# First attention of a gated cross-attention network on one core: the order of a unit's transposes and its products with V

## The chip, the cores and the metric

The kernel runs on one core of one Trainium2 chip. The time is that of one execution on the device, in microseconds (us). The engines are TensorE (PE in the profile; PEld is its loading of weights), VectorE (DVE), ScalarE (ACT), GpSimd (POOL) and SyncE (SP), which here only starts transfers. All of them run their own streams of instructions and wait for one another on semaphores that the program sets by hand.

## The reference

Four layers are computed one after the other, each added to x; the change touches the first attention only. It has 32 heads over 8 key-value heads, queries of 256 rows and keys of 768 rows, in two batches.

```python
kv = jnp.concatenate([context, latents], axis=1)
q = (latents @ Wq).reshape(bsz, q_len, HEADS, HEAD_DIM).transpose(0, 2, 1, 3)
k = (kv @ Wk).reshape(bsz, kv_len, KV_HEADS, HEAD_DIM).transpose(0, 2, 1, 3)
v = (kv @ Wv).reshape(bsz, kv_len, KV_HEADS, HEAD_DIM).transpose(0, 2, 1, 3)
q = rms_norm(q, q_norm_w)
k = rms_norm(k, k_norm_w)
scores = jnp.einsum('bhgqd,bhkd->bhgqk', qg, k) * scale
probs = jax.nn.softmax(scores.astype(jnp.float32), axis=-1).astype(q.dtype)
out = jnp.einsum('bhgqk,bhkd->bhgqd', probs, v)
...
x = x + jnp.tanh(g_xattn[0]) * _L0_xattn_ref(_layernorm(x, axis=-1), ctx_4096, ...)
```

## The kernel before, in words

Each fp32 product is made of three matmuls (`mm3`, L72 to L74): every operand is kept as a high part (`...H`, written by ACT) and a low part (`...L`, what the high part leaves out, written by DVE).

The first attention makes one turn for each of the 8 key-value heads g. A turn has 8 units u: head u // 2 of the group's four, batch u % 2. What is done for a unit, with the short names that the text uses:

- S(u): scores of unit u, 12 matmuls into the two banks `score0` and `score1`, half a unit (a query tile of 128) in each. DVE takes the maximum of each half (L443), ACT the exponential of each half (L316), into `probs`.
- T(u, j), j = 0, 1, 2: four transposes of `probs` for a third of the keys, into one bank `tbank` (L539). ACT copies the bank into `ptH` (L290; here hi(u, j)); DVE then writes `ptL` from the bank and `ptH` (L430; here lo(u, j)). The bank is free when lo(u, j) has ended.
- V(u, j): six matmuls of that third with V into `obank`.
- Q(h): four transposes of the queries of the next head, into a `tbank`, at the start of even units; `qTH` by ACT, `qTL` by DVE (L432).
- R(h): four transposes of the reciprocals of the row sums of head h, into a `tbank`. ACT copies them to `o_norm` (`factors`), DVE multiplies the head's output by them (`normalise_o`, L456), ACT copies that to `oTH` (`hi_o`, L310), POOL makes `oTL` from it (`o_lo_part`, L205).

PE's order in a unit u of `attend` is Q or R where there is one, S(u + 1), and then T(u, 0) V(u - 1, 0) T(u, 1) V(u - 1, 1) T(u, 2) V(u - 1, 2). ACT's is the copies of Q or R, hi(u, 0), an exponential, hi(u, 1), an exponential, `hi_o` in odd units from 3 on, hi(u, 2). DVE's is shown below. There are two `tbank`s, used in turn through one list `order`, and each set of transposes waits for the low part of the set two before it. There are two `obank`s, one for each second head.

At the end of a turn PE projects the queries of the next turn (`project_q`), with one tile of it ahead of the last unit's V. Its weights are split into high and low parts by POOL, which works in this order in a turn: `o_lo_part` of head 0, split of `wo`, `o_lo_part` of head 1, split of `wq` (for which SP loads the stage once `wo` has been split out of it), split of `wkv`, the rest. After it PE goes through the projections of keys and values, the transposes of K and the output product of the turn.

Of the kernel before, what the change touches and what calls it, by code (L numbers as in the profile page):

```python
# [18 lines left out]
fp32 = mybir.dt.float32  # L19
f32r = mybir.dt.float32r  # L20
bf16 = mybir.dt.bfloat16
ALU = mybir.AluOpType
ACT = mybir.ActivationFunctionType
# [22 lines left out]
def f32(ap):  # L46
    return ap.bitcast(fp32)
# [29 lines left out]
def attn0(nc, S, ctx, A):  # L77
# [23 lines left out]
    vH, vL = sb("vH", [P, NKT, D0], f32r), sb("vL", [P, NKT, D0], f32r)  # L101
    qTH, qTL = sb("qTH", [P, GRP, ROWS], f32r), sb("qTL", [P, GRP, ROWS], f32r)
    kTH, kTL = sb("kTH", [P, NKT * P], f32r), sb("kTL", [P, NKT * P], f32r)
    NP, NPT = 4, 4
    probs_mem = sb("probs", [P, NP * SKV], fp32)
    probs = probs_mem[:].rearrange("p (n k) -> p n k", n=NP)

# [6 lines left out]
    negmax, rsum = sb("negmax", [P, 16], fp32), sb("rsum", [P, 16], fp32)  # L114
    ps = S.psum_in(ctx)
    score = [ps(f"score{i}", [P, 1024], fp32) for i in range(2)]
    tbank = [ps(f"tbank{i}", [P, 512], fp32) for i in range(2)]
    obank = [ps(f"obank{i}", [P, 512], fp32) for i in range(2)]
    pbank = [score[i // 2][:, (i % 2) * 512:(i % 2 + 1) * 512] for i in range(4)]

    U, CH = 2 * GRP, 3
# [2 lines left out]
    for u in range(U):  # L124
        if u % 2 == 0 and u // 2 + 1 < GRP:
            order.append(("q", u // 2 + 1))
        if u % 2 == 1 and u >= 3:
            order.append(("r", (u - 3) // 2))
        order += [("p", CH * u + j) for j in range(CH)]
    order.append(("r", GRP - 1))  # L130
    at = {name: i for i, name in enumerate(order)}
    TC = len(order)
    NS, NKV = 2, NKT // 2
    wq_split, wkv_split, wo_split = S.wq_split, sem("wkv_split"), sem("wo_split")
    pe_q, act_q, pe_kv, act_kv, v_lo = sem("pe_q"), sem("act_q"), sem("pe_kv"), sem("act_kv"), sem("v_lo")
# [3 lines left out]
    Q_NORMED, K_NORMED = RT, [RT + 2 * i + 2 for i in range(3)]  # L139
    pe_t, t_hi, t_lo = sem("pe_t"), sem("t_hi"), sem("t_lo")  # L140
    pe_s, s_max, s_exp, r_inv = sem("pe_s"), sem("s_max"), sem("s_exp"), sem("r_inv")
    pe_pv, o_hi, o_lo = sem("pe_pv"), sem("o_hi"), sem("o_lo")
    pe_wo, x_add = sem("pe_wo"), sem("x_add")
    LAST = KVH - 1

# [6 lines left out]
    with nc.Block() as block:  # L152
# [26 lines left out]
        def _(pool):  # L179
# [7 lines left out]
            def split_wq(g):  # L187
                split(wqH[:], wqL[:], S.wqo_stage[:], S.wq_in, g, wq_split)
# [34 lines left out]
            def turn(g):  # L223

                o_lo_part(g, 0)
                split_wo(g)
                o_lo_part(g, 1)
                pool.wait_ge(pe_q, RT * g + RT)
                split_wq(g + 1)
                pool.wait_ge(pe_kv, NKV * g + NKV)  # L230
                split_wkv(g + 1)
                for h in range(2, GRP):
                    o_lo_part(g, h)
                rsqrt_items(g + 1)

            def last():
# [10 lines left out]
        def _(act):  # L247
# [39 lines left out]
            def hi(g, name, out, scale=1.0):  # L287
                c = at[name]
                act.wait_ge(pe_t, TC * g + c + 1)
                act.activation(out, tbank[c % 2][:], ACT.Copy, scale=scale).then_inc(t_hi, 1)  # L290

            def hi_q(g, h):
                hi(g, ("q", h), qTH[:, h, :], scale=S.wqk[:])
# [12 lines left out]
                hi(g, ("r", h), o_norm[:])  # L306

            def hi_o(g, h):
                act.wait_ge(t_lo, TC * g + at["r", h] + 1)
                act.activation(oTH[:, h, :], o_norm[:], ACT.Copy).then_inc(o_hi, 1)  # L310

            def exp(g, m):
# [6 lines left out]
            def attend(g):  # L319
                exp(g, 0)  # L320
                exp(g, 1)
                for u in range(U):
                    if u % 2 == 0 and u // 2 + 1 < GRP:
                        hi_q(g, u // 2 + 1)
                    if u % 2 == 1 and u >= 3:
                        factors(g, (u - 3) // 2)
                    hi_p(g, CH * u)
                    if u + 1 < U:
                        exp(g, 2 * u + 2)
                    hi_p(g, CH * u + 1)  # L330
                    if u + 1 < U:
                        exp(g, 2 * u + 3)
                    if u % 2 == 1 and u >= 3:
                        hi_o(g, (u - 3) // 2)
                    hi_p(g, CH * u + 2)
# [31 lines left out]
        def _(dve):  # L367
# [58 lines left out]
            def lo(g, name, out, hi, scale=None):  # L426
                c = at[name]
                dve.wait_ge(t_hi, TC * g + c + 1)
                if scale is None:
                    i = dve.tensor_tensor(out, tbank[c % 2][:], f32(hi), ALU.subtract)  # L430
                else:
                    i = dve.scalar_tensor_tensor(out, tbank[c % 2][:], scale, f32(hi), ALU.mult, ALU.subtract)  # L432
                i.then_inc(t_lo, 1)

            def lo_q(g, h):
# [16 lines left out]
            def normalise_o(g, h):  # L452
                c = at["r", h]
                dve.wait_ge(t_hi, TC * g + c + 1)
                dve.wait_ge(pe_pv, 24 * g + 2 * CH * (h + 1))
                dve.tensor_tensor(o_norm[:], obank[h % 2][:], o_norm[:], ALU.mult).then_inc(t_lo, 1)  # L456

            def attend(g):
                for u in range(U):
                    if u + 1 < U:  # L460
                        maximum(g, 2 * u + 2)
                    if u % 2 == 0 and u // 2 + 1 < GRP:
                        lo_q(g, u // 2 + 1)
                    if u % 2 == 1 and u >= 3:
                        normalise_o(g, (u - 3) // 2)
                    if u + 1 < U:
                        maximum(g, 2 * u + 3)
                    for c in range(CH * u, CH * u + CH):
                        lo(g, ("p", c), ptL[:, c % NPT, :], ptH[:, c % NPT, :])
                    if u % 2 == 1:  # L470
                        reciprocals(g, u // 2)

            def add_out(g, t):
                dve.wait_ge(pe_wo, RT * g + t + 1)
                dve.scalar_tensor_tensor(S.X[:, t, :], obank[t % 2][:], S.tanh_g[:, 0:1], S.X[:, t, :],
                                         ALU.mult, ALU.add).then_inc(x_add, 1)

            def turn(g):
# [30 lines left out]
        def _(pe):  # L509
# [23 lines left out]

            def transposes(g, name, ins):
                c = at[name]
                if c >= 2:
                    pe.wait_ge(t_lo, TC * g + c - 1)
                for n, block_in in enumerate(ins):
                    i = pe.transpose(tbank[c % 2][:, n * P:(n + 1) * P], block_in, S.ident[:])  # L539
                i.then_inc(pe_t, 1)  # L540

            def transpose_k(g, i):
# [12 lines left out]
            def scores(g, u):  # L555
                h, b = u // 2, u % 2
                if b == 0 and h:
                    pe.wait_ge(t_lo, TC * g + at["q", h] + 1)
                if h == 0:
                    pe.wait_ge(t_lo, TC * g + at["k", 1 + b] + 1)  # L560
                for m in (2 * u, 2 * u + 1):
                    if u:
                        pe.wait_ge(s_exp, 16 * g + m - 1)
                    q = slice(b * SQ + (m % 2) * P, b * SQ + (m % 2 + 1) * P)
                    for k0, n in ((0, 512), (512, 256)):
                        keys = slice(b * SKV + k0, b * SKV + k0 + n)
                        i = mm3(pe, score[m % 2][:, k0:k0 + n], (qTH[:, h, q], qTL[:, h, q]),
                                (kTH[:, keys], kTL[:, keys]), True, True)
                    i.then_inc(pe_s, 1)
# [7 lines left out]

            def times_v(g, u, j):
                h, b, c = u // 2, u % 2, CH * u + j
                if u % 2 == 0 and j == 0 and h >= 2:  # L580
                    pe.wait_ge(t_lo, TC * g + at["r", h - 2] + 1)
                pe.wait_ge(t_lo, TC * g + at["p", c] + 1)
                for kt in range(2):
                    key = b * KVT + 2 * j + kt
                    part = slice(kt * 256, (kt + 1) * 256)
                    i = mm3(pe, obank[h % 2][:, b * SQ:(b + 1) * SQ], (vH[:, key, :], vL[:, key, :]),
                            (ptH[:, c % NPT, part], ptL[:, c % NPT, part]), j == 0 and kt == 0, j == CH - 1 and kt == 1)
                i.then_inc(pe_pv, 1)

            def attend(g):  # L590

                for u in range(U):
                    if u % 2 == 0 and u // 2 + 1 < GRP:
                        transpose_q(g, u // 2 + 1)
                    if u % 2 == 1 and u >= 3:
                        transpose_factors(g, (u - 3) // 2)
                    if u + 1 < U:
                        scores(g, u + 1)
                    for j in range(CH):
                        transpose_probs(g, u, j)  # L600
                        if u:
                            times_v(g, u - 1, j)

            def finish_units(g):
                for j in range(CH):
                    times_v(g, U - 1, j)
                transpose_factors(g, GRP - 1)

            def output(g, t):
                if t == 0:  # L610
# [3 lines left out]
                    pe.wait_ge(x_add, RT * g + t - 1)  # L614
                rows = slice(t * P, (t + 1) * P)
                for h in range(GRP):
                    i = mm3(pe, obank[t % 2][:], (oTH[:, h, rows], oTL[:, h, rows]),
                            (woH[:, h, :], woL[:, h, :]), h == 0, h == GRP - 1)
                i.then_inc(pe_wo, 1)

# [1015 lines left out]
```

## Time and profile before

| | us |
|---|---|
| median of 3 runs | 1085.82 |
| lowest, highest | 1079.99, 1086.55 |
| the profiled execution's own time | 1088.03 |
| its span in the trace | 1086.2 |
| PE busy | 1005.9 |
| DVE busy | 632.7 |
| ACT busy | 501.4 |
| POOL busy | 359.8 |

The seven turns of the loop repeat every 94 us or so, from about 64 us to 724 us of the span; the eighth stands behind the loop. A row of the timeline gives the start, the duration and, in brackets, how long the engine was idle before it and what released it. The duration of a matmul runs from its start to its modelled end; the next one starts before that, so that the pace is read from the starts. Adjacent instructions on ACT and DVE overlap by about 0.1 us in the same way.

### The profile page before, as it was taken

Reading aid. Unit: us, or ns where it says so; the run is one execution under the profiler, and the core shown is the slowest. Engines: PE = TensorE matmul, PEld = TensorE weight load, DVE = VectorE, ACT = ScalarE, POOL = GpSimd, SP = SyncE. Lnnn points to the kernel's source line nnn. Section 1 sums busy time; section 2 is a strip of 40 time slices with the busy share of each in tenths; the row PEclk is TensorE's granted clock in tenths of the full one; section 3 lists DMA queues with packets and bytes.
Section 4 is the critical chain, followed back from the end, with each engine's and each line's share of the span. In section 5 each row is a group of like instructions: output and inputs, shape, how many; then the busy total and the mean of one; then the engine's idle time right before and its main releaser. Section 6 shows DMA issues by size and latency. Waiting matters only on the chain. (4 is left out here: it accounts for less than half of the span.)

```text
span 1086.2 us, 18566 instructions
## 1 busy us (share of the span) xinstructions
PE 1005.9 (93%) x6748; PEld 878.6 (81%) x6748; DVE 632.7 (58%) x1102; ACT 501.4 (46%) x968; POOL 359.8 (33%) x246
## 2 busy tenths in 40 slices
PE   4899999999999999999999999999899969999975
PEld 3888989898898989889898898989677857777654
DVE  6566457556546745754674574567347736666464
ACT  4356337435534643653473374346145125555423
POOL 3307403720830371083046126305147308000041
PEclk9989999999999999999999999999999989999987
DMA  6001100200200110020011003000053072221001
GB/s 213 2 1 62 37 1 9 88 0 0 90 6 0 38 59 0 0 97 0 0 58 39 0 0 116 0 1 1 26 179 116 1 237 56 54 53 34 2 0 39
DMA packets 31409, 46.49 MB, mean 43 GB/s; under 512 B 3472, under 2 KB 15376, under 8 KB 31376
## 3 DMA queue, kind: packets, MB, share of 16 engines
q1 hardware_dynamic: 30800, 46.03, 13.6%
q8 instruction: 22, 0.36, 0.1%
q14 instruction: 11, 0.09, 0.0%
q10 hardware_dynamic: 576, 0.00, 0.0%
HBM read 41.83 MB, written 4.19 MB: 42 GB/s over the span
## 5 line engine op out<-in xcount | busy, mean ns | idle before, releaser
L430 DVE TENSOR_TENSOR ptL<-tbank,ptH 128x512 fp32r<-128x512 f32 x192 | 132.3, 689 | 84.0 <-ACT ptH L290 84.0
L290 ACT ACTIVATE ptH<-tbank 128x512 fp32r<-128x512 f32 x192 | 115.7, 603 | 109.5 <-PE tbank L539 109.2
L205 POOL TENSOR_TENSOR oTL<-o_norm,oTH 128x512 fp32r<-128x512 f32 x32 | 41.3, 1290 | 349.9 <-ACT oTH L310 349.9
L539 PE MATMUL tbank<-ident,probs 128*128 128x128 f32 x864 | 132.1, 275 | 16.5 <-DVE ptL L430 12.1
L443 DVE TENSOR_REDUCE negmax<-score 128x1 f32<-128x768 f32 x128 | 119.5, 949 | 19.9 <-PE score L74 19.9
L316 ACT ACTIVATE probs<-score,negmax 128x768 f32<-128x768 f32 x128 | 115.6, 904 | 15.5 <-DVE negmax L443 15.5
L72 PE MATMUL obank<-ptH,vH 128*128 128x256 f32 x384 | 122.3, 318 | 0.0
L401 DVE TENSOR_REDUCE sumsq<-probs 128x2 f32<-128x256 f32 (+1 forms) x80 | 42.0, 526 | 135.5 <-ACT probs L285 71.8
L539 PEld LDWEIGHTS tbank<-ident,probs 128*128 128x128 f32 x864 | 97.7, 140 | 26.5 <-DVE ptL L430 14.9
L74 PE MATMUL obank<-ptH,vL 128*128 128x256 f32 x384 | 108.8, 283 | 0.0
L1419 DVE TENSOR_REDUCE a_negmax<-a_score 128x1 fp32r<-128x512 f32 x128 | 82.3, 685 | 45.3 <-PE a_score L1472 44.5
L74 PE MATMUL score<-wkvH,kvT_lo 128*128 128x256 f32 x384 | 108.7, 283 | 0.0
L73 PE MATMUL score<-wkvL,kvT_hi 128*128 128x256 f32 x384 | 108.7, 283 | 0.0
L72 PE MATMUL score<-wkvH,kvT_hi 128*128 128x256 f32 x384 | 108.6, 283 | 0.0
L73 PE MATMUL obank<-ptL,vH 128*128 128x256 f32 x384 | 108.4, 282 | 0.0
L200 POOL TENSOR_TENSOR rnorm<-sumsq,neg_half 128x2 f32<-128x2 f32 (+1 forms) x80 | 71.4, 896 | 107.4 <-DVE sumsq L403 107.3
L1400 ACT ACTIVATE a_exp<-a_scoreT 128x1024 f32<-128x1024 f32 x64 | 65.6, 1025 | 60.2 <-PE a_scoreT L1489 60.2
L72 PE MATMUL score<-kTH,qTH 128*128 128x512 f32 (+1 forms) x256 | 92.4, 361 | 0.6 <-DVE kTL L430 0.6
L74 PE MATMUL score<-kTH,qTL 128*128 128x512 f32 (+1 forms) x256 | 87.2, 341 | 0.0
L73 PE MATMUL score<-kTL,qTH 128*128 128x512 f32 (+1 forms) x256 | 87.2, 341 | 0.0
L72 PEld LDWEIGHTS obank<-ptH,vH 128*128 128x128 f32 x384 | 73.6, 192 | 0.5
L72 PEld LDWEIGHTS score<-wkvH,kvT_hi 128*128 128x128 f32 x384 | 73.7, 192 | 0.3
(246 smaller groups left out, 2417.6 us busy)
## 6 DMA issues: line engine op xcount, KB each, us to landing
wqo_stage<-in_wq SPq DMA_DIRECT2D x9, 1024.0 KB, 5.6
wqo_stage<-in_wo SPq DMA_DIRECT2D x8, 1024.0 KB, 5.2
wkv_stage<-in_wkv SPq DMA_DIRECT2D x9, 512.0 KB, 6.4
a_qS<-q_scratch SPq DMA_DIRECT2D x24, 128.0 KB, 3.6
ctx_stage<-in_ctxT SPq DMA_DIRECT2D x2, 1024.0 KB, 12.5
kS<-k_scratch SPq DMA_DIRECT2D x32, 64.0 KB, 2.1
q_scratch<-qpart SPq DMA_DIRECT2D x16, 128.0 KB, 1.9
wqo_stage<-in_down_w SPq DMA_DIRECT2D x3, 512.0 KB, 3.5
```

The costliest lines, as they stand in the source:

```text
L72: pe.matmul(out, a[0], b[0], start=start, stop=False)
L73: pe.matmul(out, a[0], b[1], start=False, stop=False)
L74: return pe.matmul(out, a[1], b[0], start=False, stop=stop)
L200: pool.tensor_tensor(rn[:, GRP * it:GRP * it + n], ss[:, GRP * it:GRP * it + n], S.neg_half[:, 0:n], ALU.pow).then_inc(rn_done, 1)
L290: act.activation(out, tbank[c % 2][:], ACT.Copy, scale=scale).then_inc(t_hi, 1)
L316: act.activation(probs[:, m % NP, :], score[m % 2][:, 0:SKV], ACT.Exp, bias=negmax[:, m:m + 1], accum_out=rsum[:, m:m + 1]).then_inc(s_exp, 1)
L401: dve.tensor_reduce(ss[:, a:a + n], sq[:, it % 3, 0:n], AX.X, ALU.add).then_inc(ss_done, 1)
L430: i = dve.tensor_tensor(out, tbank[c % 2][:], f32(hi), ALU.subtract)
L443: dve.tensor_reduce(negmax[:, m:m + 1], score[m % 2][:, 0:SKV], AX.X, ALU.max, negate=True).then_inc(s_max, 1)
L539: i = pe.transpose(tbank[c % 2][:, n * P:(n + 1) * P], block_in, S.ident[:])
L1400: act.activation(expo[:, v % NE_, :], scoreT[v % 2][:], ACT.Exp).then_inc(s_exp, 1)
L1419: dve.tensor_reduce(negmax[:, 2 * (v % 2) + t:2 * (v % 2) + t + 1], score[t][:], AX.X, ALU.max, negate=True).then_inc(s_max, 1)
```

## The change

The order on PE within a unit becomes Q and R, S(u + 1), T(u, 0), T(u, 1), T(u, 2), and then V(u - 1, 0), V(u - 1, 1), V(u - 1, 2). For this there are three `tbank`s and one `obank` (the output product uses `obank` and `tbank2` in turn). A list `place` gives each set its bank: Q in `tbank1`, R in `tbank2`, T(u, j) in `tbank` j. Each set waits for whoever used its own bank last (`user`): for the low part, or, behind R, for ACT's copy. R(h) is transposed one unit sooner, in the even unit 2h + 2, behind Q. The product of DVE with the factors gets a semaphore of its own (`o_scaled`), and stands first in its odd unit. The single `obank` makes V(u - 1, 0) wait for that product. `ptH` and `ptL` have five buffers in place of four. At the turn's end R(3) goes ahead of the last unit's V, and POOL makes the low part of head 2 ahead of the split of `wkv`.

```diff
     kTH, kTL = sb("kTH", [P, NKT * P], f32r), sb("kTL", [P, NKT * P], f32r)
-    NP, NPT = 4, 4
+    NP, NPT = 4, 5
     probs_mem = sb("probs", [P, NP * SKV], fp32)
...
     score = [ps(f"score{i}", [P, 1024], fp32) for i in range(2)]
-    tbank = [ps(f"tbank{i}", [P, 512], fp32) for i in range(2)]
-    obank = [ps(f"obank{i}", [P, 512], fp32) for i in range(2)]
+    tbank = [ps(f"tbank{i}", [P, 512], fp32) for i in range(3)]
+    obank = ps("obank", [P, 512], fp32)
+    wbank = [obank, tbank[2]]
...
         if u % 2 == 0 and u // 2 + 1 < GRP:
             order.append(("q", u // 2 + 1))
-        if u % 2 == 1 and u >= 3:
-            order.append(("r", (u - 3) // 2))
+        if u % 2 == 0 and u:
+            order.append(("r", u // 2 - 1))
         order += [("p", CH * u + j) for j in range(CH)]
     order.append(("r", GRP - 1))
     at = {name: i for i, name in enumerate(order)}
     TC = len(order)
+
+    lows = {name: i for i, name in enumerate(name for name in order if name[0] != "r")}
+    TL = len(lows)
+
+    place = [n if kind == "p" and n < CH else {"p": n % CH, "q": 1, "k": c % 2, "r": 2}[kind] if c else 0
+             for c, (kind, n) in enumerate(order)]
+    user = [max((i for i in range(c) if place[i] == place[c]), default=None) for c in range(TC)]
     NS, NKV = 2, NKT // 2
     wq_split, wkv_split, wo_split = S.wq_split, sem("wkv_split"), sem("wo_split")
...
                 split_wq(g + 1)
+                o_lo_part(g, 2)
                 pool.wait_ge(pe_kv, NKV * g + NKV)
                 split_wkv(g + 1)
-                for h in range(2, GRP):
-                    o_lo_part(g, h)
+                o_lo_part(g, 3)
                 rsqrt_items(g + 1)
 
...
                 act.wait_ge(pe_t, TC * g + c + 1)
-                act.activation(out, tbank[c % 2][:], ACT.Copy, scale=scale).then_inc(t_hi, 1)
+                act.activation(out, tbank[place[c]][:], ACT.Copy, scale=scale).then_inc(t_hi, 1)
 
...
             def hi_o(g, h):
-                act.wait_ge(t_lo, TC * g + at["r", h] + 1)
+                act.wait_ge(o_scaled, GRP * g + h + 1)
                 act.activation(oTH[:, h, :], o_norm[:], ACT.Copy).then_inc(o_hi, 1)
 
...
                     if u % 2 == 0 and u // 2 + 1 < GRP:
                         hi_q(g, u // 2 + 1)
-                    if u % 2 == 1 and u >= 3:
-                        factors(g, (u - 3) // 2)
+                    if u % 2 == 0 and u:
+                        factors(g, u // 2 - 1)
                     hi_p(g, CH * u)
                     if u + 1 < U:
...
                 if scale is None:
-                    i = dve.tensor_tensor(out, tbank[c % 2][:], f32(hi), ALU.subtract)
+                    i = dve.tensor_tensor(out, tbank[place[c]][:], f32(hi), ALU.subtract)
                 else:
-                    i = dve.scalar_tensor_tensor(out, tbank[c % 2][:], scale, f32(hi), ALU.mult, ALU.subtract)
+                    i = dve.scalar_tensor_tensor(out, tbank[place[c]][:], scale, f32(hi), ALU.mult, ALU.subtract)
                 i.then_inc(t_lo, 1)
 
...
                 dve.wait_ge(t_hi, TC * g + c + 1)
                 dve.wait_ge(pe_pv, 24 * g + 2 * CH * (h + 1))
-                dve.tensor_tensor(o_norm[:], obank[h % 2][:], o_norm[:], ALU.mult).then_inc(t_lo, 1)
+                dve.tensor_tensor(o_norm[:], obank[:], o_norm[:], ALU.mult).then_inc(o_scaled, 1)
 
             def attend(g):
                 for u in range(U):
+                    if u % 2 == 1 and u >= 3:
+                        normalise_o(g, (u - 3) // 2)
                     if u + 1 < U:
                         maximum(g, 2 * u + 2)
                     if u % 2 == 0 and u // 2 + 1 < GRP:
                         lo_q(g, u // 2 + 1)
-                    if u % 2 == 1 and u >= 3:
-                        normalise_o(g, (u - 3) // 2)
                     if u + 1 < U:
                         maximum(g, 2 * u + 3)
+                    if u % 2 == 1:
+                        reciprocals(g, u // 2)
                     for c in range(CH * u, CH * u + CH):
                         lo(g, ("p", c), ptL[:, c % NPT, :], ptH[:, c % NPT, :])
-                    if u % 2 == 1:
-                        reciprocals(g, u // 2)
 
             def add_out(g, t):
                 dve.wait_ge(pe_wo, RT * g + t + 1)
-                dve.scalar_tensor_tensor(S.X[:, t, :], obank[t % 2][:], S.tanh_g[:, 0:1], S.X[:, t, :],
+                dve.scalar_tensor_tensor(S.X[:, t, :], wbank[t % 2][:], S.tanh_g[:, 0:1], S.X[:, t, :],
                                          ALU.mult, ALU.add).then_inc(x_add, 1)
 
...
             def transposes(g, name, ins):
                 c = at[name]
-                if c >= 2:
-                    pe.wait_ge(t_lo, TC * g + c - 1)
+                if name == ("p", 2):
+                    pe.wait_ge(t_lo, TL * g + lows["q", 1] + 1)
+                elif user[c] is not None:
+                    last_user = order[user[c]]
+                    if last_user in lows:
+                        pe.wait_ge(t_lo, TL * g + lows[last_user] + 1)
+                    else:
+                        pe.wait_ge(t_hi, TC * g + at[last_user] + 1)
                 for n, block_in in enumerate(ins):
-                    i = pe.transpose(tbank[c % 2][:, n * P:(n + 1) * P], block_in, S.ident[:])
+                    i = pe.transpose(tbank[place[c]][:, n * P:(n + 1) * P], block_in, S.ident[:])
                 i.then_inc(pe_t, 1)
 
...
             def times_v(g, u, j):
                 h, b, c = u // 2, u % 2, CH * u + j
-                if u % 2 == 0 and j == 0 and h >= 2:
-                    pe.wait_ge(t_lo, TC * g + at["r", h - 2] + 1)
-                pe.wait_ge(t_lo, TC * g + at["p", c] + 1)
+                if u % 2 == 0 and j == 0 and h:
+                    pe.wait_ge(o_scaled, GRP * g + h)
+                pe.wait_ge(t_lo, TL * g + lows["p", c] + 1)
                 for kt in range(2):
                     key = b * KVT + 2 * j + kt
                     part = slice(kt * 256, (kt + 1) * 256)
-                    i = mm3(pe, obank[h % 2][:, b * SQ:(b + 1) * SQ], (vH[:, key, :], vL[:, key, :]),
+                    i = mm3(pe, obank[:, b * SQ:(b + 1) * SQ], (vH[:, key, :], vL[:, key, :]),
                             (ptH[:, c % NPT, part], ptL[:, c % NPT, part]), j == 0 and kt == 0, j == CH - 1 and kt == 1)
...
                     if u % 2 == 0 and u // 2 + 1 < GRP:
                         transpose_q(g, u // 2 + 1)
-                    if u % 2 == 1 and u >= 3:
-                        transpose_factors(g, (u - 3) // 2)
+                    if u % 2 == 0 and u:
+                        transpose_factors(g, u // 2 - 1)
                     if u + 1 < U:
                         scores(g, u + 1)
                     for j in range(CH):
                         transpose_probs(g, u, j)
-                        if u:
+                    if u:
+                        for j in range(CH):
                             times_v(g, u - 1, j)
 
             def finish_units(g):
+                transpose_factors(g, GRP - 1)
                 for j in range(CH):
                     times_v(g, U - 1, j)
-                transpose_factors(g, GRP - 1)
 
             def output(g, t):
```

PE, unit 2 of a turn (the low parts are counted by `t_lo`, ACT's copies by `t_hi`). Before, S(3) is past, and T(2, j) and V(1, j) stand in turn, up to R(0), the first thing of unit 3:

```order
L539 MATMUL tbank0<-ident,probs 128x128 [waits t_lo]
...
L72 MATMUL obank1<-ptH,vH 128x256 [waits t_lo]
...
L539 MATMUL tbank1<-ident,probs 128x128 [waits t_lo]
...
L72 MATMUL obank1<-ptH,vH 128x256 [waits t_lo]
...
L539 MATMUL tbank0<-ident,probs 128x128 [waits t_lo]
...
L72 MATMUL obank1<-ptH,vH 128x256 [waits t_lo]
...
L539 MATMUL tbank1<-ident,rsum 128x128 [waits t_lo]
```

After, from Q(2) and R(0) at the head of unit 2, across S(3), to T(2, 0), T(2, 1), T(2, 2) and the first product, up to S(4):

```order
L553 MATMUL tbank1<-ident,q_rows 128x128 [waits t_lo]
...
L553 MATMUL tbank2<-ident,rsum 128x128 [waits t_lo]
...
L72 MATMUL score0<-kTH,qTH 128x512 [waits s_exp]
...
L553 MATMUL tbank0<-ident,probs 128x128 [waits t_lo]
...
L553 MATMUL tbank1<-ident,probs 128x128 [waits t_lo]
...
L553 MATMUL tbank2<-ident,probs 128x128 [waits t_hi]
...
L72 MATMUL obank<-ptH,vH 128x256 [waits t_lo]
...
L72 MATMUL score0<-kTH,qTH 128x512 [waits s_exp]
```

The transposes no longer have products between them, and R(0) stands ahead of S(3), with a wait for the low part of the last user of `tbank2`, which is T(1, 2).

DVE, from the last low part of unit 2 through unit 3. Before:

```order
L430 TENSOR_TENSOR ptL<-tbank0,ptH 128x512 [waits t_hi]
...
L443 TENSOR_REDUCE negmax<-score0 128x1 [waits pe_s]
...
L456 TENSOR_TENSOR o_norm<-obank1,o_norm 128x512 [waits pe_pv]
...
L443 TENSOR_REDUCE negmax<-score1 128x1 [waits pe_s]
...
L430 TENSOR_TENSOR ptL<-tbank0,ptH 128x512 [waits t_hi]
...
L430 TENSOR_TENSOR ptL<-tbank1,ptH 128x512 [waits t_hi]
...
L430 TENSOR_TENSOR ptL<-tbank0,ptH 128x512 [waits t_hi]
```

After:

```order
L438 TENSOR_TENSOR ptL<-tbank2,ptH 128x512 [waits t_hi]
...
L464 TENSOR_TENSOR o_norm<-obank,o_norm 128x512 [waits pe_pv]
...
L451 TENSOR_REDUCE negmax<-score0 128x1 [waits pe_s]
...
L451 TENSOR_REDUCE negmax<-score1 128x1 [waits pe_s]
...
L438 TENSOR_TENSOR ptL<-tbank0,ptH 128x512 [waits t_hi]
...
L438 TENSOR_TENSOR ptL<-tbank1,ptH 128x512 [waits t_hi]
...
L438 TENSOR_TENSOR ptL<-tbank2,ptH 128x512 [waits t_hi]
```

The product with the factors has moved ahead of both maxima, and the reciprocals ahead of the unit's low parts.

## Rows read from the trace of the kernel before

**Rows 1.** The page: busy time of the engines, and PE's in 40 slices:

```profile
PE 1005.9 (93%) x6748; PEld 878.6 (81%) x6748; DVE 632.7 (58%) x1102; ACT 501.4 (46%) x968; POOL 359.8 (33%) x246
...
PE   4899999999999999999999999999899969999975
```

**Rows 2.** Busy time in four stretches: start:end, length, engines, PEclk, DMA share, GB/s:

```profile
249.90:252.70 2.80, 1.78 (x15) 1.30 (x13) 2.39 (x5) 2.12 (x5) 0.00 (x0) 1.00 0.00 0
254.00:348.00 94.00, 90.51 (x616) 82.56 (x615) 54.65 (x95) 44.79 (x95) 34.55 (x20) 0.98 0.08 28
295.70:299.10 3.40, 3.40 (x9) 2.64 (x8) 0.00 (x0) 0.00 (x0) 3.32 (x3) 0.50 0.86 297
348.00:442.00 94.00, 90.54 (x626) 82.79 (x625) 55.59 (x96) 46.27 (x100) 34.58 (x20) 1.00 0.09 28
```

**Rows 3.** Timeline of PE, turn from 249.94: start, us, line, operation, count, [idle before]:

```profile
252.22 0.66 PE L539 MATMUL tbank<-ident,probs 128*128 128x128 f32 x4 [0.81 <-DVE ptL L430]
...
254.80 0.60 PE L539 MATMUL tbank<-ident,probs 128*128 128x128 f32 x4
...
258.26 0.60 PE L539 MATMUL tbank<-ident,q_rows 128*128 128x128 f32 x4
...
260.81 0.60 PE L539 MATMUL tbank<-ident,probs 128*128 128x128 f32 x4
261.17 0.36 PE L72 MATMUL obank<-ptH,vH 128*128 128x256 f32 x1
261.37 0.28 PE L73 MATMUL obank<-ptL,vH 128*128 128x256 f32 x1
...
261.97 0.60 PE L539 MATMUL tbank<-ident,probs 128*128 128x128 f32 x4
...
266.83 0.60 PE L539 MATMUL tbank<-ident,probs 128*128 128x128 f32 x4
...
292.61 0.28 PE L74 MATMUL obank<-ptH,vL 128*128 128x256 f32 x1
294.66 0.50 PE L72 MATMUL score<-wqH,kvT_hi 128*128 128x512 f32 x1 [1.78 <-POOL wqL L185]
```

**Rows 4.** One line, L539: duration of its transposes in ns, min/median/max:

```profile
L539 PE MATMUL tbank<-ident,probs x864: 270/272/417, 49.1 to 762.1; 128*128 128x128 f32 x173
```

**Rows 5.** Timeline of ACT in the same turn:

```profile
253.20 0.22 ACT L316 ACTIVATION_READ_ACCUMULATOR probs<-score,negmax 128x1 f32 x1
...
263.29 0.91 ACT L316 ACTIVATE probs<-score,negmax 128x768 f32<-128x768 f32 x1
...
264.17 0.61 ACT L290 ACTIVATE ptH<-tbank 128x512 fp32r<-128x512 f32 x1
...
270.19 0.65 ACT L310 ACTIVATE oTH<-o_norm 128x512 fp32r<-128x512 f32 x1
```

**Rows 6.** Timeline of DVE in the same turn:

```profile
260.83 0.74 DVE L432 SCALAR_TENSOR_TENSOR qTL<-tbank,wqk,qTH 128x512 fp32r<-128x512 f32 x1
...
263.45 0.69 DVE L430 TENSOR_TENSOR ptL<-tbank,ptH 128x512 fp32r<-128x512 f32 x1 [0.41 <-ACT ptH L290]
264.81 0.69 DVE L430 TENSOR_TENSOR ptL<-tbank,ptH 128x512 fp32r<-128x512 f32 x1 [0.67 <-ACT ptH L290]
...
271.35 0.69 DVE L430 TENSOR_TENSOR ptL<-tbank,ptH 128x512 fp32r<-128x512 f32 x1 [1.19 <-ACT ptH L290]
```

**Rows 7.** Timeline of POOL in the same turn:

```profile
270.91 1.30 POOL L205 TENSOR_TENSOR oTL<-o_norm,oTH 128x512 fp32r<-128x512 f32 x1 [36.12 <-ACT oTH L310]
...
290.05 4.56 POOL L185 TENSOR_TENSOR wqL<-wqo_stage,wqH 128x2048 fp32r<-128x2048 f32 x1
```

**Rows 8.** Timeline of all engines after the last turn's attention:

```profile
765.11 0.60 PE L539 MATMUL tbank<-ident,rsum 128*128 128x128 f32 x4
...
766.43 0.69 DVE L456 TENSOR_TENSOR o_norm<-obank,o_norm 128x512 f32<-128x512 f32 x1 [2.53 <-ACT o_norm L290]
...
769.27 0.47 PE L72 MATMUL obank<-woH,oTH 128*128 128x512 f32 x1 [3.56 <-POOL oTL L205]
```

More of the change, by code:

```diff
@@ L141, in attn0 @@
     pe_s, s_max, s_exp, r_inv = sem("pe_s"), sem("s_max"), sem("s_exp"), sem("r_inv")
-    pe_pv, o_hi, o_lo = sem("pe_pv"), sem("o_hi"), sem("o_lo")
+    pe_pv, o_scaled, o_hi, o_lo = sem("pe_pv"), sem("o_scaled"), sem("o_hi"), sem("o_lo")
     pe_wo, x_add = sem("pe_wo"), sem("x_add")
@@ L557, in scores @@
                 if b == 0 and h:
-                    pe.wait_ge(t_lo, TC * g + at["q", h] + 1)
+                    pe.wait_ge(t_lo, TL * g + lows["q", h] + 1)
                 if h == 0:
-                    pe.wait_ge(t_lo, TC * g + at["k", 1 + b] + 1)
+                    pe.wait_ge(t_lo, TL * g + lows["k", 1 + b] + 1)
                 for m in (2 * u, 2 * u + 1):
@@ L616, in output @@
                 for h in range(GRP):
-                    i = mm3(pe, obank[t % 2][:], (oTH[:, h, rows], oTL[:, h, rows]),
+                    i = mm3(pe, wbank[t % 2][:], (oTH[:, h, rows], oTL[:, h, rows]),
                             (woH[:, h, :], woL[:, h, :]), h == 0, h == GRP - 1)
```

## The prediction

> **What bounds the kernel now.** I read the page first: PE is busy 93% of the span, DVE 58%, ACT 46%, and PE's digits are nines through all the turns [rows 1]. A turn of 94.0 us has 90.5 us of PE in it [rows 2], so that PE's own work bounds the turn, and only some 3.5 us of a turn are idle. The change takes no matmul away. It can gain by a faster pace of the same matmuls or by filling those 3.5 us, and lose by any new wait of PE longer than the ones it removes. The timeline of PE shows where the idle time stands: 0.81 us ahead of T(0, 2), and 1.78 us ahead of the projection of queries, which waits for POOL's split of its weights [rows 3]. The timelines of ACT, DVE and POOL say when a bank comes free and what POOL's split hangs on [rows 5 to 7]. All times below are from one turn, in which T(0, 0) starts at 249.94.
>
> **Does grouping make PE faster?** The row of the first product after a transpose reads 0.36, the others 0.28, and its successor starts 0.20 later instead of 0.12 [rows 3]. That looks like 0.08 us for each change from transposes to products. The starts say otherwise. A set of four transposes covers 0.60 us and one lasts 0.272 [rows 3, 4], so they start (0.60 - 0.272) / 3 = 0.109 apart. From the start of a set at 260.81 to the second product at 261.37 are 0.56 = 4 x 0.109 + 0.12: four transposes and one product at their own pace, with nothing for the change. The gain of grouping is therefore taken as 0; if the 0.08 were real it would be 14 changes fewer in a turn (two in each of seven units), 1.1 us, and the bound on that side. Sizes used below: a set 0.44, three sets 1.31; T(2, 0) to T(2, 1) with V(1, 0) between is 1.16 [rows 3], so a V is 0.72 and three are 2.16; S(3), from Q at 258.26 plus 0.44 to T(2, 0) at 260.81, is 2.11.
>
> **When the banks come free.** Counted from the start of T(u, 0), called 0:
> - lo(u, 1) ends at 263.45 + 0.69 - 260.81 = 3.33, lo(u, 2) at 264.81 + 0.69 - 260.81 = 4.69 [rows 3, 6].
> - In the odd units 3 and 5 ACT has `hi_o` ahead of hi(u, 2) [rows 5], and lo(3, 2) ends at 271.35 + 0.69 - 266.83 = 5.21.
> - These times are paced by ACT (two copies and two exponentials, one after the other, then the third copy, which starts in the row at 264.17 as the exponential of 263.29 ends [rows 5]) and not by PE, so issuing T(u, 1) and T(u, 2) earlier doesn't move them. A wait ends about 0.04 later.
>
> **R's new place.** After the change the products of unit u end 1.31 + 2.16 = 3.47 after T(u, 0). Then come Q in `tbank1`, whose last user ended at 3.33: no wait. R in `tbank2` wants to start at 3.91 and must wait for lo(u, 2): until 4.73 behind unit 1 (0.82 of wait), until 5.25 behind unit 3 (1.34), and behind unit 5, where there is no Q and it wants to start at 3.47, until 5.25 (1.78). Queued behind R on PE is S(u + 1), and behind that everything. Before, the same R stood in the odd unit and asked for the set two before it, lo(u - 1, 1), at 3.33: covered by the products. ACT's copy of R(2) also waits for POOL's low part of head 1, which ends at 270.91 + 1.30 - 266.83 = 5.38 after T(5, 0) [rows 3, 7]; R's transposes end later than that, so it is covered by some 0.3.
>
> **T(u, 1) behind Q.** It needs `qTL`, which ended at 260.83 + 0.74, 2.87 after the start of S [rows 3, 6]. T(u, 0) starts 2.11 after that, T(u, 1) wants 2.55 and gets 2.91: 0.36 of wait in units 2 and 4. Before, V(u - 1, 0) covered it. In unit 0 nothing was there to cover it in either kernel.
>
> **Unit 0 gains.** T(0, 2) has a bank of its own, so its wait of 0.81 goes. What is late next is the exponential: S(2)'s second half waits for one that is read out at 253.20 + 0.22 [rows 5], and takes 1.06 (half an S), so T(1, 0) starts at 254.53 instead of 254.80 [rows 3]: 0.27 gained.
>
> **The sum for a turn.** T(2, 0) = T(1, 0) + 4.73 + 0.44 + 2.11 = 254.53 + 7.28 = 261.81. T(3, 0) = that + 0.80 + 0.87 + 2.16 + 2.11 = 267.75, 0.92 later than before. T(4, 0) = + 5.25 + 0.44 + 2.11 = 275.55. T(5, 0) = + 5.94 = 281.49. T(6, 0) = + 7.80 = 289.29. T(7, 0) follows the products, 3.47 later, but T(7, 2) waits for lo(6, 2), at 4.73, and V(6, 0) for DVE's product with R(2), which runs behind lo(6, 2): 4.69 + 0.69 [rows 8], less the overlap of 0.08 between two instructions, + 0.04 = 5.34. V(6, 2) ends at 289.29 + 5.34 + 2.16 = 296.79; before it ended at 292.61 + 0.12 = 292.73. That is 4.06 later. In the turn 1.93 of it (292.73 to 294.66) is hidden, because the projection waited that long for POOL. POOL's chain starts with `hi_o` of head 0 in unit 3 [rows 5, 7], so it comes 0.92 later and would let PE go at 295.58: earlier than 296.79. The projection starts at 296.79 instead of 294.66, 2.13 later. From there to the turn's end PE has no wait of weight, and POOL's reordered low part (1.3 us) has the four query projections in front of whoever needs `wkv`, so that 2.13 is paid in full.
>
> **The last turn** has no projection: it pays 4.06, and gets something back, because R(3) now goes ahead of the last V. DVE's product started at 766.43, 1.32 after R(3) at 765.11 [rows 8]; now it follows the last V, which ends 0.44 later than before and completes about 0.2 after that: 0.7 gained. Net 3.4.
>
> Sum: 7 x 2.13 + 3.4 = 18.3. From the profiled execution, 1088.0 + 18.3 = 1106.3; that one lies 2.2 above the median of the three runs, so the **forecast is 1104 us**.
>
> **The clock.** In the turn from 254 to 348 the granted clock was at 0.50, which is 1.2 GHz, for 3.4 us right behind the wait for POOL; the next turn, with the same wait, kept 1.00 (2.4 GHz) [rows 2]. Such a stretch costs at most 3.4 / 2 = 1.7. Three of the seven turns have one. After the change that wait is gone, and 1.78 ahead of R(2) is there, in eight turns. I take as many as before, so 0; bounds are -5 (none is left) and +8 (all eight fall). The Trainium skill, page "TensorE: Matmul & The Clock Gate", Part 4, says that transposes do not count as PE work for this clock, which speaks against three sets in a row. By the rows of unit 0, a stretch of 2.80 us with transposes as nearly all of its work and 1.02 idle ran at 1.00 [rows 2], so here the rule adds no chance beyond the third rival.
>
> **Rivals.**
> 1. *R does not bind: no slower than before.* If lo(u, 2) ended by 3.9 instead of 4.69 and 5.21, R would slip into the pace. That needs hi(u, 2) about 0.8 to 1.3 sooner, for instance if ACT's copies and exponentials ran closer once all three banks are filled. Then T(3, 0) is 0.1 later than before, the products of unit 6 end under POOL's cover at about 292.8, and the turn is 0.1 longer: 1085.8 + 0.7 - 0.7 = 1086. For it: three banks are full early. Against: ACT has no wait between these steps now, so it has nothing to catch up. 8%.
> 2. *The change from transposes to products does cost 0.08.* Then V(1), V(3) and V(5), which lie between R's waits, shorten by 0.16 each: 0.5 a turn, 18.3 - 8 x 0.5 = 14.3, 1100. Even then slower. 10%, with a weaker gap ahead of R in the same case: 1092 to 1099.
> 3. *The clock falls at each of the longer gaps of R.* Two gaps (1.34 and 1.78) in eight turns at 1.7, less the 5 of now: + 22 on top, 1126. For it: the 1.78. Against: four of seven such gaps did nothing, and the 1.34 is shorter. 7%.
> 4. *A real gain.* Rival 1 and the 0.08 together are capped by POOL, whose chain moves by only 0.24: 7 x 0.24 + 1 = 3 less, 1083, still within 1%. To be faster by over 1% something must speed up that no row shows. 3%.
>
> **The numbers.** The forecast case, 1099 to 1113, has 72%: its bounds are the clock's, -5 and +8. With the second rival's 1092 and some above 1113 the range is 1092 to 1115; outside lie rivals 1, 3 and 4, 18%. A measurement of this kernel tells about 1%, so the bounds are 1075 and 1097. Faster 3%; the same 15% (rival 1 and the lower part of rival 2); slower 82%.
>
> **What the profile of after would show.** PE idle 0.7, 1.2 and 1.6 us (less the tail of the last matmul) ahead of the transposes of `rsum`, released by DVE's `ptL`, in units 2, 4 and 6; 0.2 to 0.4 ahead of T(2, 1) and T(4, 1), released by `qTL`; no wait for POOL's `wqL` at the projection; turns of 96 us; twelve transposes in 1.31 us and eighteen products in 2.16. I am wrong if R starts without a wait, if the pitch of transposes or products differs in longer runs, if the clock stays at half in attention, or if POOL still holds the projection.

## The result, and the profile after

| | before | after |
|---|---|---|
| median, us | 1084.03 (4 runs) | 1104.15 (4 runs) |
| lowest, highest | 1079.99, 1086.55 | 1103.39, 1106.59 |
| the profiled execution | 1088.03, span 1086.2 | 1104.61, span 1102.8 |

The ratio after to before is 1.0189, with a 95% interval of 1.0161 to 1.0216: the change makes the kernel 1.9% slower. The forecast was 1104.

The page of the changed kernel: busy time of the engines, PE's in 40 slices, and the granted clock of TensorE in tenths. The work is the same as before [rows 1]; PE is busy for 4 us more in the records and idle for 12 more.

```profile
PE 1010.1 (92%) x6748; PEld 873.0 (79%) x6748; DVE 633.9 (57%) x1102; ACT 500.5 (45%) x968; POOL 360.0 (33%) x246
...
PE   4898999999899999999989999998899969999975
...
PEclk9999999999999999999999999999999989999988
```

Two stretches of the changed kernel, a little over one turn each, with the columns of [rows 2]. From projection to projection a turn takes 95.87 us, against 93.4 in the kernel before where the clock doesn't fall, and the granted clock is 1.00 in both stretches.

```profile
257.00:354.00 97.00, 92.36 (x627) 83.03 (x626) 55.91 (x96) 46.66 (x100) 34.62 (x20) 1.00 0.08 27
354.00:450.00 96.00, 91.44 (x622) 82.34 (x622) 55.22 (x95) 45.64 (x98) 34.67 (x20) 1.00 0.08 27
```

The timeline of PE in the turn whose T(0, 0) starts at 254.36, 4.42 later than in the turn shown of before [rows 3]. The waits that the prediction named are in brackets.

```profile
255.18 1.09 PE L553 MATMUL tbank<-ident,probs 128*128 128x128 f32 x8 [0.21 <-DVE qTL L440]
256.53 0.50 PE L72 MATMUL score<-kTH,qTH 128*128 128x512 f32 x1 [0.26 <-ACT probs L324]
...
259.06 1.47 PE L553 MATMUL tbank<-ident,probs 128*128 128x128 f32 x12
260.28 0.36 PE L72 MATMUL obank<-ptH,vH 128*128 128x256 f32 x1
260.48 0.28 PE L73 MATMUL obank<-ptL,vH 128*128 128x256 f32 x1
...
263.81 0.65 PE L553 MATMUL tbank<-ident,rsum 128*128 128x128 f32 x4 [0.69 <-DVE ptL L438]
...
266.39 0.60 PE L553 MATMUL tbank<-ident,probs 128*128 128x128 f32 x4
267.22 1.09 PE L553 MATMUL tbank<-ident,probs 128*128 128x128 f32 x8 [0.23 <-DVE qTL L440]
...
272.41 1.47 PE L553 MATMUL tbank<-ident,probs 128*128 128x128 f32 x12
...
277.68 0.65 PE L553 MATMUL tbank<-ident,rsum 128*128 128x128 f32 x4 [1.21 <-DVE ptL L438]
...
291.55 0.65 PE L553 MATMUL tbank<-ident,rsum 128*128 128x128 f32 x4 [1.65 <-DVE ptL L438]
...
301.62 0.28 PE L74 MATMUL obank<-ptH,vL 128*128 128x256 f32 x1
301.74 0.39 PE L72 MATMUL score<-wqH,kvT_hi 128*128 128x512 f32 x1
```

Read it downwards. The eight transposes at 255.18 are T(0, 1) and T(0, 2): the wait of 0.81 between them is gone, and 0.26 for the exponential stands ahead of S(2) instead. At 259.06 twelve transposes start, at 260.28 the first product, at 260.48 the second: 1.42 us, which is 12 x 0.109 + 0.12. At 263.81, 277.68 and 291.55 stand R(0), R(1) and R(2), with 0.69, 1.21 and 1.65 of idle time ahead of them, released by DVE's `ptL`. At 267.22 T(2, 1) has waited for `qTL`. The last product at 301.62 is followed by the projection at 301.74 with no wait for POOL; in [rows 3] there was one of 1.78.

DVE in the same turn: `ptL` of the third set of units 1, 3 and 5, which R waits for, and `qTL` (266.42).

```profile
263.06 0.69 DVE L438 TENSOR_TENSOR ptL<-tbank,ptH 128x512 fp32r<-128x512 f32 x1 [0.68 <-ACT ptH L298]
...
266.42 0.74 DVE L440 SCALAR_TENSOR_TENSOR qTL<-tbank,wqk,qTH 128x512 fp32r<-128x512 f32 x1
...
276.93 0.69 DVE L438 TENSOR_TENSOR ptL<-tbank,ptH 128x512 fp32r<-128x512 f32 x1 [1.20 <-ACT ptH L298]
...
290.81 0.69 DVE L438 TENSOR_TENSOR ptL<-tbank,ptH 128x512 fp32r<-128x512 f32 x1 [1.19 <-ACT ptH L298]
```

They end at 263.75, 277.62 and 291.50, and R starts 0.05 to 0.06 later each time.

### The profile page after: what moved, and what is told of

The parts are those of the page before. It is cut to its first block and busy times, and to the rows that moved or that the text cites. A ratio compares the mean times of both kernels' runs of the same rounds, so it can differ in the third digit from the quotient of the medians.

```text
span 1102.8 us, 18559 instructions
## 1 busy us (share of the span) xinstructions
PE 1010.1 (92%) x6748; PEld 873.0 (79%) x6748; DVE 633.9 (57%) x1102; ACT 500.5 (45%) x968; POOL 360.0 (33%) x246
## 5 line engine op out<-in xcount | busy, mean ns | idle before, releaser
L553 PE MATMUL tbank<-ident,probs 128*128 128x128 f32 x864 | 116.8, 276 | 8.4 <-DVE qTL L440 8.0
L72 PE MATMUL obank<-ptH,vH 128*128 128x256 f32 x384 | 113.9, 297 | 0.0
```

The source lines that it names most:

```text
L72: pe.matmul(out, a[0], b[0], start=start, stop=False)
L553: i = pe.transpose(tbank[place[c]][:, n * P:(n + 1) * P], block_in, S.ident[:])
```

## The experiments

The turn is the start of one turn's first query projection to the next one's, from the timeline of PE. In the kernel before it is 93.2 to 93.5 us where the clock doesn't fall, and 94.5 and 94.9 in the two turns with a fall of the clock in them (a third fall comes in the eighth turn); the turns of each kernel below are alike within 0.06 us, but for those with a fall and one of 93.32 with R behind the scores. Theory A, the prediction's, is that R ahead of the scores waits for the third low part of the unit before. Theory B puts the loss on the grouping itself, theory C on POOL's chain, which starts later. Each ratio is to runs of the kernel before taken beside it: their median is 1084.03 us for the changed kernel, 1084.65 for the next four rows and 1084.25 for the last four.

| kernel | median, us | ratio to before, 95% interval | turn, us |
|---|---|---|---|
| changed | 1104.15 | 1.0189 (1.0161 to 1.0216) | 95.87 |
| R behind the scores | 1086.10 | 1.0013 (1.0001 to 1.0026) | 93.08 |
| qTL first | 1097.35 | 1.0117 (1.0092 to 1.0143) | 94.97 |
| T and V in turn | 1105.12 | 1.0179 (1.0151 to 1.0207) | 95.83 |
| hi_o first | 1096.62 | 1.0113 (1.0082 to 1.0144) | 94.83 |
| R behind the scores, hi_o first | 1064.26 | 0.9804 (0.9770 to 0.9837) | 90.90 |
| before, hi_o early | 1072.44 | 0.9881 (0.9850 to 0.9912) | 91.82 |
| R behind, hi_o first, T and V in turn | 1069.51 | 0.9862 (0.9833 to 0.9890) | 91.68 |
| T and V in turn but for unit 7 | 1094.65 | 1.0088 (1.0060 to 1.0115) | 94.97 |

**R behind the scores.** One step of the change is put elsewhere, all the rest stays.

```diff
-                    if u % 2 == 0 and u:
-                        transpose_factors(g, u // 2 - 1)
                     if u + 1 < U:
                         scores(g, u + 1)
+                    if u % 2 == 0 and u:
+                        transpose_factors(g, u // 2 - 1)
```

> The changed kernel with one edit: R(h) is transposed behind S(u + 1) instead of ahead of it; grouping, three banks, one obank all stay. Theory A (the loss is R's wait for lo(u, 2), ahead of the scores): behind the scores R wants its bank 6.0 after the last T(u, 0), and lo(u, 2) ends by 5.2, so the waits of 0.7, 1.2 and 1.65 go, and those of 0.23 ahead of T(2, 1) and T(4, 1) too, which R's transposes now cover. A turn falls from 95.9 to about 93.2 and the projection waits for POOL again (about 2 us), with some falls of the clock behind it: 1084 to 1088. Theory B (the loss is in the grouping itself): no more than a few us, 1098 to 1104.

Measured 1086.10, and the loss is gone. The timeline of PE, S(3), R(0), the twelve transposes of unit 2 and the projection of this turn:

```profile
257.32 0.28 PE L74 MATMUL score<-kTH,qTL 128*128 128x256 f32 x1
257.44 0.60 PE L553 MATMUL tbank<-ident,rsum 128*128 128x128 f32 x4
257.87 1.51 PE L553 MATMUL tbank<-ident,probs 128*128 128x128 f32 x12
...
291.22 0.50 PE L72 MATMUL score<-wqH,kvT_hi 128*128 128x512 f32 x1 [1.90 <-POOL wqL L193]
```

R(0) at 257.44 follows the scores at their pace, and the transposes follow R: neither R's wait nor the one for `qTL` ahead of T(2, 1) is left. The projection waits for POOL again, 1.90. Two stretches of this kernel, a turn and the 3.4 us just behind such a wait:

```profile
257.00:350.00 93.00, 90.52 (x614) 81.94 (x612) 53.64 (x94) 44.38 (x96) 34.60 (x20) 0.98 0.09 28
292.60:296.00 3.40, 3.40 (x11) 2.60 (x10) 0.00 (x0) 0.40 (x1) 3.32 (x2) 0.50 0.83 297
```

The clock is at 0.50 there, as in [rows 2], in three of the seven turns. Theory B, that the grouping is at fault, has fallen: all of it is in this kernel.

**qTL first** on DVE, ahead of the first maximum of an even unit:

```diff
+                    if u % 2 == 0 and u // 2 + 1 < GRP:
+                        lo_q(g, u // 2 + 1)
                     if u + 1 < U:
                         maximum(g, 2 * u + 2)
-                    if u % 2 == 0 and u // 2 + 1 < GRP:
-                        lo_q(g, u // 2 + 1)
```

> The changed kernel with one edit on DVE: qTL ahead of the unit's first maximum instead of behind it. Both theories: the wait ahead of T(2, 1) and T(4, 1) goes (0.42 from start to start, two a turn, eight turns), 6.7 less: 1097 to 1098. If the maxima, which come 0.7 later only where qTL was not yet due, delay an exponential, less is gained.

Measured 1097.35, with turns 0.90 shorter. DVE had been idle there for 1.79 us, waiting for the scores.

**hi_o first** on ACT, in the odd unit where it was idle for 2.7 us:

```diff
+                    if u % 2 == 1 and u >= 3:
+                        hi_o(g, (u - 3) // 2)
                     hi_p(g, CH * u)
...
-                    if u % 2 == 1 and u >= 3:
-                        hi_o(g, (u - 3) // 2)
                     hi_p(g, CH * u + 2)
```

> The changed kernel with one edit on ACT: hi_o stands first in its odd unit, where ACT is idle, instead of ahead of hi(u, 2). Theory A: lo(3, 2) and lo(5, 2) end 0.52 sooner, so R waits 0.52 less in units 4 and 6: 1.04 a turn, 8.3 in eight turns, 1096. POOL's chain starts 3 us sooner, which changes nothing, since the projection doesn't wait for it. Theory C (POOL's chain still paces the turn): 3 us a turn less, some 1083. Theory B: no change, 1104.

Measured 1096.62, with turns 1.04 shorter: R(1) and R(2) wait 0.52 less each, and R(0), which has no hi_o ahead of it, as long as before.

```profile
260.13 0.65 PE L553 MATMUL tbank<-ident,rsum 128*128 128x128 f32 x4 [0.68 <-DVE ptL L438]
...
273.48 0.65 PE L553 MATMUL tbank<-ident,rsum 128*128 128x128 f32 x4 [0.69 <-DVE ptL L438]
...
286.83 0.65 PE L553 MATMUL tbank<-ident,rsum 128*128 128x128 f32 x4 [1.13 <-DVE ptL L438]
```

The copy that starts POOL's chain came 4.0 us sooner (17.4 us after T(0, 0) instead of 21.4), and the turn won no more than R's two waits, so theory C has fallen: in the changed kernel PE paces the turn.

**T and V in turn**, as before, with everything else as in the change:

```diff
                     for j in range(CH):
                         transpose_probs(g, u, j)
-                    if u:
-                        for j in range(CH):
+                        if u:
                             times_v(g, u - 1, j)
```

> The changed kernel with one edit on PE: T(u, j) and V(u - 1, j) stand in turn again; R's place, the three banks and the one obank stay. Theory A: the waits of R stay as they are, since lo(u, 2) is paced by ACT; the wait ahead of T(u, 1) is covered by V(u - 1, 0) again: 6.7 less, 1097 to 1098, the same as with qTL first. Theory B, and the rival by which each change from transposes to products costs 0.08: grouping pays, so that this one is 4 to 9 us above the one with qTL first, 1101 to 1106.

Measured 1105.12, where theory A had 1097 to 1098: a miss, and within the rival's 1101 to 1106. But the timeline does not show the rival's mechanism. Unit 7 of a turn:

```profile
295.89 0.65 PE L553 MATMUL tbank<-ident,probs 128*128 128x128 f32 x4
297.62 0.38 PE L72 MATMUL obank<-ptH,vH 128*128 128x256 f32 x1 [1.08 <-DVE o_norm L464]
...
298.44 0.60 PE L553 MATMUL tbank<-ident,probs 128*128 128x128 f32 x4
...
299.59 0.60 PE L553 MATMUL tbank<-ident,probs 128*128 128x128 f32 x4
...
300.74 0.39 PE L72 MATMUL score<-wqH,kvT_hi 128*128 128x512 f32 x1
```

From one set of transposes to the next, with a V between, are 1.15 us (298.44 to 299.59), and three such pairs are 3.45; grouped, twelve transposes and eighteen products of the changed kernel take 3.46 (259.06 to Q at 262.52). So a change from transposes to products costs nothing. What is new is the 1.08 ahead of V(6, 0), which waits for DVE's product out of the only `obank`. T(7, 1) and T(7, 2) stood inside this wait in the grouped order; here they are behind it. T(7, 0) starts 42.49 us after T(0, 0) instead of 43.39, which is 0.90 won in units 2 and 4; the projection starts 47.34 after it instead of 47.38, so that 0.86 is lost again in unit 7.

**T and V in turn but for unit 7** was made to tell this wait from a cost of going from transposes to products.

> The changed kernel with T and V in turn in units 1 to 6 and grouped in unit 7. If the loss of the version in turn order is all in unit 7, where V(6, 0) waits for the single obank and the transposes behind it with it, this one keeps the gain of units 2 and 4 (0.42 each): 1097 to 1098, as with qTL first. If there is a cost of changing between transposes and products (0.08), it stays at 1101 or more.

Measured 1094.65, turns of 94.97, to 0.01 us those of the kernel with qTL first. So the miss was the single bank's wait in unit 7, and the pace of PE is the same in either order. The median lies 2.4 below the 1097 that was expected and 2.7 below that of the kernel with qTL first, though the turns are equal. The two profiled executions took 1097.58 and 1097.43; three of the four runs here had a mean granted clock of 0.984, the four with qTL first 0.979 to 0.982. So the difference goes with the clock of the runs, and not with the order.

**R behind the scores and hi_o first**, the two edits together:

> The changed kernel with two edits: R behind the scores, and hi_o first in its odd unit. With R behind the scores alone PE was ready about 2.2 us before POOL's split of wq at the projection of each turn. hi_o of head 0 starts POOL's chain, and it comes some 3.5 us sooner here. Theory A: the projection then goes when PE is ready, 2.2 less in seven turns, and the three falls of the clock behind the wait (1.6 each) go as well: 1066, below both kernels. If POOL's chain hangs on something else (the transfer of the stage, the low part of head 1), it stays near 1086.

Measured 1064.26, 2.0% below the kernel before (0.9804, 0.9770 to 0.9837) and 40 us below the changed one. POOL's chain in one turn, its start and its end:

```profile
260.71 1.28 POOL L213 TENSOR_TENSOR oTL<-o_norm,oTH 128x512 fp32r<-128x512 f32 x1 [32.37 <-ACT oTH L318]
...
279.76 4.59 POOL L193 TENSOR_TENSOR wqL<-wqo_stage,wqH 128x2048 fp32r<-128x2048 f32 x1
```

It ends at 284.35. The projection in the same turn starts when the last product is issued, with no wait:

```profile
285.80 0.28 PE L74 MATMUL obank<-ptH,vL 128*128 128x256 f32 x1
285.92 0.39 PE L72 MATMUL score<-wqH,kvT_hi 128*128 128x512 f32 x1
```

The clock stays at full speed through the seven turns of the loop.

**The kernel before, hi_o early**, with the old order, two `tbank`s and two `obank`s:

```diff
                     hi_p(g, CH * u)
+                    if u % 2 == 1 and u >= 3:
+                        hi_o(g, (u - 3) // 2)
                     if u + 1 < U:
                         exp(g, 2 * u + 2)
...
-                    if u % 2 == 1 and u >= 3:
-                        hi_o(g, (u - 3) // 2)
```

> The kernel before with one edit on ACT: hi_o directly behind hi(u, 0) of its odd unit instead of ahead of hi(u, 2). It comes 2.2 us sooner. Theory A: the wait of 1.8 for POOL goes in seven turns (12.6), with three falls of the clock (4.8); the exponentials of unit 3 come 0.5 later, so Q(3) waits about 0.45 (3.6 in eight turns): 1070 to 1072. It says how much of a gain is to be had with the old order of PE.

Measured 1072.44. No projection waits for POOL any more, and the clock doesn't fall in the seven turns. Q(3) pays for it with a wait for lo(3, 1), which comes later; one row of PE:

```profile
265.44 0.65 PE L539 MATMUL tbank<-ident,q_rows 128*128 128x128 f32 x4 [0.28 <-DVE ptL L430]
```

By the medians, twelve of the twenty us that the best kernel wins over before can thus be had by hi_o's place alone, in the old order. The other 8 come with the changed order; hi_o can stand first in its unit only because R is transposed a unit sooner. How much of the 8 the third `tbank` gives by itself was not tried.

**The best kernel with T and V in turn** asks what the grouping is worth in it.

> The kernel with R behind the scores and hi_o first, with T(u, j) and V(u - 1, j) in turn again. The changed kernel in turn order lost in unit 7 what it won in units 2 and 4: V(6, 0) waited 1.08 for DVE's product out of the single obank, and two sets of transposes stood behind it (0.87 a turn). The same here, with nothing won elsewhere: 0.87 in eight turns, 7 above the grouped one, 1073. If grouping matters in the other units as well, it is more.

Measured 1069.51, where 1073 was expected, with turns 0.78 longer than those of the best kernel (0.87 expected). V(6, 0) waits for the single `obank` as above:

```profile
284.98 0.39 PE L72 MATMUL obank<-ptH,vH 128*128 128x256 f32 x1 [1.08 <-DVE o_norm L464]
```

Grouping is worth 5 us there by the medians, not by a faster PE but because transposes stand ahead of a wait that would hold them up. In the profiled executions the output product of the last turn starts at 753.3 us here, at 753.6 in the old order with hi_o early, and at 747.2 in the best kernel. So with a single `obank`, the third `tbank` and R's new place gave nothing beyond hi_o's place until the sets were grouped. Whether the old order with two `obank`s would gain by grouping was not tried.

## Why the prediction was right

Step by step, for the turn shown; measured times have 4.42 taken off.

| step | predicted | measured |
|---|---|---|
| T(1, 0) | 254.53 | 254.64 |
| R(0), 4.73 later | 259.26 | 259.39 |
| T(2, 0) | 261.81 | 261.97 |
| T(3, 0) | 267.75 | 267.99 |
| the projection | 296.79 | 297.32 |

- **Grouping gives no pace.** Right: the longer duration of the first product's record is no cost. The second rival had taken it for one; it fell with the 1.42 us above, and with the equal turns of two kernels in either order.
- **R binds.** Right, in its place, its cause (ACT's pace sets lo(u, 2), the transposes' time of issue doesn't) and its size: 0.7, 1.2 and 1.6 of idle were named, 0.69, 1.21 and 1.65 came. Putting R behind the scores undid it, and 0.52 less of ACT's work ahead of it gave back 0.52 for each R. The first rival, that R would slip in, fell.
- **T(2, 1) behind Q.** Right in kind; it costs 0.39 from start to start, not 0.36 (267.22 - 266.39 = 0.83, where 0.44 is the pace), and `qTL` first gave back 0.45 for each of the two.
- **The sum for a turn.** The turn grew by 2.5 where 2.13 stood. The projection is 0.53 later than worked out, and that is many small ones: the eight steps from T(0, 0) to the projection are each 0.02 to 0.11 longer than worked out.
- **The clock.** The term was taken as 0 and was about -4 in the profiled executions: the three falls behind the wait for POOL went, and none came for R's gaps, of up to 1.65 in the loop and 1.80 in the eighth turn. This offset the too small turn. The third rival fell. With R behind the scores the wait for POOL is back, and so are three falls; with hi_o early in the old order the wait is gone, and the falls with it. That the falls come with that wait is shown this way. The length of the wait alone doesn't decide it: the six falls stood behind waits of 1.78 to 2.09, and eight other projections of the two kernels waited 1.39 to 2.00 without one. What does decide it stays open. Two rows of PE, R(2) in the eighth turn of the changed kernel, with no fall, and a projection with R behind the scores, with one:

```profile
771.25 0.62 PE L553 MATMUL tbank<-ident,rsum 128*128 128x128 f32 x4 [1.80 <-DVE ptL L438]
```

```profile
479.30 0.50 PE L72 MATMUL score<-wqH,kvT_hi 128*128 128x512 f32 x1 [2.09 <-POOL wqL L193]
```

The Trainium skill's rule in "TensorE: Matmul & The Clock Gate", Part 4 (transposes don't count as PE work for the clock) was given no weight beside the row; twelve transposes in a row ran in eight turns without a fall. That does not refute the rule, since products and scores lie on both sides.
- **The last turn** grew by about 4 net of a fall (102.19 against 99.60 from the last projection to the output product, with a fall of some 1.4 in the old one), where 3.4 stood. Behind the attention of the last turn the work is the same, yet the profiled execution of after was 1.6 shorter there. From the start of the output product to the end, before and after, with the columns of [rows 2]:

```profile
769.27:1086.20 316.93, 283.81 (x1820) 218.99 (x1820) 178.97 (x320) 125.06 (x173) 80.61 (x73) 0.94 0.24 68
```

```profile
787.41:1102.80 315.39, 281.67 (x1820) 216.96 (x1820) 178.71 (x320) 125.05 (x173) 80.69 (x73) 0.95 0.24 69
```

This goes with the clock. In the profiled executions of all the kernels here the same stretch takes 314.5 to 318.8 us, the shortest at a granted clock of 0.96 and the longest at 0.94. Why the clock differs there is not shown.

In the two profiled executions the growth is 16.6 where 18.3 stood. Against that sum it has roughly 2.6 more for the turns, 0.6 more for the last, 0.9 more because the first projection starts later (19.36 against 18.48), 4.2 less for the falls and 1.6 less behind attention. Between the medians it is 20.1. The forecast added 18.3 to a median of 1085.8, which with a fourth run became 1084.0: the growth was 1.8 too small and the base 1.8 too large. That the total of 1104 hit so closely is luck; its terms did not. The prediction's mechanism, not the last digit, is what the runs bear out. What it left out is that the same change opens the way to a gain, with R 2.1 us further down and hi_o first in its unit, so that POOL's chain begins sooner. R's place alone only brought the time back to that of before.

## What to carry to other kernels

When a set of work is moved ahead in an in-order stream, write down for its buffer who used it last and when that user ends, counted from the point that paces that user. If the user is paced by a third engine, issuing its input earlier moves nothing, and the wait stands in front of all that is queued behind. Judge a possible cost of switching between kinds of matmul by start-to-start times over a whole group, not by the duration in the first one's row. Where an engine off the path (here POOL) starts a long chain from one small instruction, put that instruction where its engine is idle; one instruction moved by 2.2 us gave 1.2%, and together with the changed order and R behind the scores 2.0%.

## What the runs showed of the hardware

- The granted clock fell to 0.50 for 3.4 us behind six of the fourteen waits for POOL at the projection, in the kernel before and in the one with R behind the scores. These six waits were 1.78 to 2.09 us long, the other eight 1.39 to 2.00. In the seven turns of the eight other kernels, the changed one among them, PE's idle times were 1.66 or less, and the clock never fell. In all ten it fell at the last output product, which waited 2.95 to 3.56. One fall made its turn 1.2 to 1.7 us longer (94.5 and 94.9 against 93.4, 94.8 against 93.1).
- The stretch from the last output product to the end, with the same work in every kernel, took from 314.5 us (granted clock 0.96) to 318.8 (0.94). Totals that differ by up to some 4 us can differ by this alone.
- Transposes of 128 x 128 start 0.109 us apart both in sets of four between products and in runs of twelve, and a product of 256 columns starts 0.12 after its predecessor behind either.
